# Feed-forward weights rounded in the key and value stage instead of the first cross-attention

## The chip, the core and the metric

The kernel runs on one core of one Trainium2 chip. The metric is device time in microseconds (us) from the start to the end of one execution; a kernel's time is the median of its runs.

## What is computed

The reference takes `x` (256 tokens of 1024) and a context of 4096 tokens, and adds six sublayers to `x`: a cross-attention to the context and the tokens (16 query heads, 4 key heads of width 96), a causal self-attention, a small routed layer, a second cross-attention to the context (32 heads of 32), a second causal self-attention, and a feed-forward layer on whole numbers. Only the last one's weights matter here:

```python
def _quant_w(W):
    ws = jnp.max(jnp.abs(W), axis=1, keepdims=True) / QMAX
    ws = jnp.maximum(ws, 1e-08)
    Wq = jnp.clip(jnp.round(W / ws), -QMAX, QMAX)
    return (Wq, ws)
...
gate = jnp.einsum('td,id->ti', q, Wgq) * s * wsg.T
up = jnp.einsum('td,id->ti', q, Wuq) * s * wsu.T
h = jax.nn.silu(gate) * up
q2, s2 = _quant_act(h)
out = jnp.einsum('ti,di->td', q2, Wdq) * s2 * wsd.T
```

`Wg` and `Wu` are 2752 x 1024, `Wd` is 1024 x 2752, all float32. Each row has its own scale, and the rows must be divided by it and rounded. The matmuls need the rounded weights turned (contraction on the partitions). None of this depends on `x`, so it can be done at any time before the last stage.

## The kernel before

**Key and value stage** (`latent_stage`). After the queries of the first cross-attention (16 heads, L416) come 17 chunks of 256 tokens. For each, PE multiplies the chunk by the key and value weights, each float32 operand split into a high and a low part, so three matmuls for each product (L449 to L451 for keys, L468 for values), and between them scores each finished key tile against the queries once, in the high part only, for the row maxima (L436). DVE takes the maxima (L601) and the low parts of keys (L614) and values (L623, L631); ACT takes the high parts (L547, L558). At a chunk's start ACT and DVE split the next chunk's context (`c_high` L489, `c_low` L499). `chunk_steps` is one list of steps that all engines walk through, each doing its own part: "mm" and "vmm" are matmul steps, "k" and "v" take a finished tile out of PSUM, "max" is a score and its maximum. The SP queue issues every transfer, strictly in that order: two context loads (L663, four `staged` tiles in turn), four key stores after each of the first two key tiles and two after the third (L685 to L692), three value stores after each of two value tiles (L698, L701). `bank_read`, counted by DVE, tells PE that a PSUM bank is free, and SP that a tile may be stored. POOL does nothing here.

**First cross-attention** (`cross_stage`). 136 steps, 34 for each of 4 key heads. In a step PE does six matmuls of scores (`scores`, L809 to L811) and six that weigh the values (`weigh`, L824 to L826); ACT computes two exponentials (L862, L863), DVE the low part of the probabilities (`probs_low`, L900). After each head DVE inverts the sums and normalises (`normalise`, L909 to L919), in the middle of its queue. Beside this the feed-forward weights are rounded, by the table `quant`: rows of 128 are loaded (`load_rows`, L1036), DVE finds each row's largest value (`find_top`, L941, and for `Wd` L947 and L933) and its scale and inverse (L925, L927), POOL multiplies and rounds in two passes (L1008, L1014), PE turns the result in 128 x 128 pieces (`turn`, L839), DVE copies them out of PSUM (`copy_turned`, L964) and SP spills them to scratch memory (`spill`, L1045 to L1051). In the last steps four units of the output projection's weights are split (L260, L265).

**Feed-forward stage** (`whole_number_stage`). Six chunks of gate and up weights, 512 wide and the last 192, are read back (`sp_chunk`, L2045, L2049) into two buffers, then multiplied for two tiles of tokens (`gate_and_up`, L2123); `down` is read back at once (L2278) and used by `project` (L2149).

## Time and profile before

| | us |
|---|---|
| median of 3 runs (2109.82 to 2115.65) | 2112.91 |
| the profiled execution | 2105.75 |
| its span, first to last instruction | 2104.4 |
| busy in the span: PE | 1920.4 (91%) |
| DVE | 1287.9 (61%) |
| ACT | 859.5 (41%) |
| POOL | 547.6 (26%) |
| DMA, mean rate | 123 GB/s |

The key and value stage runs from about 80 to 656 us of the span, the first cross-attention from 662.7 to 1093.2 us, the feed-forward stage from about 2010 us to the end. PE's busy time counts modelled, overlapping ends of matmuls, so the distance from one start to the next tells more than a duration. "Releaser" is what an engine waited for last. The granted clock is PE's, 1.00 for full speed. The trace of a DMA has its issue on the SP queue and its landing.

### The profile page before, as it was taken

To read this page: it belongs to the slowest core of one execution; us is meant where nothing else is said; L and a number is where in the kernel's file an instruction comes from. 1 tells how busy PE (TensorE), PEld (TensorE's weight loads), DVE (VectorE), ACT (ScalarE), POOL (GpSimd) and SP (SyncE) were. 2 spreads that over 40 slices of the span, in tenths; PEclk is the share of its full clock that TensorE was granted. 3 is DMA by queue.
4 is the path that set the end of the run, shared out by engine and by line. 5 is a ranking of instruction groups with operands and counts; after the bars stand their busy time and mean duration, and the time that the engine had idled before them with its cause. 6 is when DMAs were issued, how large, how long until landed. Compare 5 with 4: busy or idle time off the path is not lost.

```text
span 2104.4 us, 29620 instructions
## 1 busy us (share of the span) xinstructions
PE 1920.4 (91%) x11932; PEld 1411.2 (67%) x11932; DVE 1287.9 (61%) x1590; ACT 859.5 (41%) x1409; POOL 547.6 (26%) x264
## 2 busy tenths in 40 slices
PE   7899999999997999999998995779999999978977
PEld 5799999999996877787776874423333333366843
DVE  3445444454544787889965855667777775266465
ACT  2211111111113666666663451046777777535421
POOL 0000000000001555554510001036777777510000
PEclk9999999999998999999999998879999999999889
DMA  4533434343326666565724516523433420135052
GB/s 173 173 105 106 125 95 117 98 123 89 88 76 177 203 201 195 189 210 189 237 73 152 188 43 160 125 80 78 96 81 81 94 61 1 38 117 224 1 189 74
DMA packets 154808, 259.30 MB, mean 123 GB/s; under 512 B 36477, under 2 KB 102321, under 8 KB 147505
## 3 DMA queue, kind: packets, MB, share of 16 engines
q1 hardware_dynamic: 154673, 257.42, 40.6%
q8 instruction: 95, 1.56, 0.3%
q14 instruction: 40, 0.33, 0.1%
HBM read 192.39 MB, written 61.76 MB: 121 GB/s over the span
## 4 chain that ended last, share of the span: by engine, by line
PE 81%; DVE 11%; ACT 3%; issue 3%; DMA 2%; SPq 0%; POOL 0%; ACTq 0%; DVEq 0%
PE psum L468 10%; PE psum L1699 7%; PE psum L1716 5%; PE psum L449 4%; PE psum L451 4%; PE psum L450 4%; PE psum L436 3%; DVE top L1888 3%; PE psum L278 3%; PE psum L279 3%; PE psum L280 3%; PE psum L1732 3%; PE psum L809 3%; PE psum L1680 3%; PE psum L811 3%; PE psum L810 3%
## 5 line engine op out<-in xcount | busy, mean ns | idle before, releaser
L1888 DVE TENSOR_REDUCE top<-psum 128x4 f32<-128x2048 f32 x128 | 293.0, 2289 | 118.5 <-PE psum L1680 118.3
L1958 POOL TENSOR_TENSOR added<-probs_f 128x1024 f32<-128x1024 f32 x126 | 299.0, 2375 | 193.6 <-ACT probs_f L1815 141.8
L1815 ACT ACTIVATE probs_f<-psum 128x512 f32<-128x512 f32 x512 | 278.4, 594 | 139.3 <-PE psum L1699 127.1
L601 DVE TENSOR_REDUCE top<-psum 128x2 f32<-128x512 f32 x272 | 186.4, 691 | 198.3 <-PE psum L436 198.2
L900 DVE TENSOR_TENSOR probs_low<-probs,probs_high 128x1024 fp32r<-128x1024 f32 x136 | 195.1, 1438 | 79.1 <-ACT probs L863 78.9
L862 ACT ACTIVATE probs_high<-psum 128x1024 fp32r<-128x1024 f32 x136 | 139.9, 1029 | 160.0 <-PE psum L811 150.3
L1699 PE MATMUL psum<-q_rows,k_rows 97*128 97x512 f32 x512 | 197.5, 461 | 0.7 <-ACT probs_f L1815 0.5
L1699 PEld LDWEIGHTS psum<-q_rows,k_rows 97*128 97x128 f32 x512 | 80.7, 191 | 171.6 <-ACT probs_f L1815 159.1
L449 PE MATMUL psum<-c_high,w_high 128*128 128x256 f32 (+1 forms) x672 | 191.4, 285 | 3.2 <-issue 3.2
L450 PE MATMUL psum<-c_low,w_high 128*128 128x256 f32 (+1 forms) x672 | 191.3, 285 | 0.0
L451 PE MATMUL psum<-c_high,w_low 128*128 128x256 f32 (+1 forms) x672 | 191.0, 284 | 0.0
L1008 POOL TENSOR_SCALAR wf_rows<-wf_rows,w_inverse 128x1024 f32<-128x1024 f32 (+2 forms) x52 | 128.8, 2477 | 186.0 <-DVE w_inverse L927 186.0
L1001 POOL MEMSET key_high<- 1x512 f32 x4 | 1.9, 520 | 653.7 <-DVE top_low L637 653.7
L1716 PE MATMUL psum<-probs_f,v_pair 128*32 128x512 f32 x1024 | 139.9, 619 | 0.2 <-ACT probs_f L1815 0.2
L863 ACT ACTIVATE probs<-psum 128x1024 f32<-128x1024 f32 x136 | 138.5, 1018 | 0.0
L449 PEld LDWEIGHTS psum<-c_high,w_high 128*128 128x128 f32 (+1 forms) x672 | 129.1, 192 | 3.6 <-issue 3.6
L450 PEld LDWEIGHTS psum<-c_low,w_high 128*128 128x128 f32 (+1 forms) x672 | 129.2, 192 | 0.0
L451 PEld LDWEIGHTS psum<-c_high,w_low 128*128 128x128 f32 (+1 forms) x672 | 129.1, 192 | 0.0
L468 PE MATMUL psum<-w_high,c_high 128*128 128x384 f32 (+1 forms) x528 | 122.4, 310 | 0.0
L468 PE MATMUL psum<-w_high,c_low 128*128 128x384 f32 (+1 forms) x528 | 122.0, 309 | 0.0
L468 PE MATMUL psum<-w_low,c_high 128*128 128x384 f32 (+1 forms) x528 | 121.9, 309 | 0.0
L809 PE MATMUL psum<-q_high,key_high 97*128 97x512 f32 x272 | 114.1, 420 | 8.3 <-DMA value_low<-v_low 8.3
(357 smaller groups left out, 3806.3 us busy)
## 6 DMA issues: line engine op xcount, KB each, us to landing
wf_rows<-in_ffn_w_dram SPq DMA_DIRECT2D x42, 512.0 KB, 4.2
staged<-in_ctxT_dram SPq DMA_DIRECT2D x32, 512.0 KB, 4.7
k_four<-k_high SPq DMA_DIRECT2D x128, 128.0 KB, 3.3
wf_rows<-in_ffn_w_dram SPq DMA_DIRECT2D x8, 1376.0 KB, 7.4
q_dram<-wf_turned SPq DMA_DIRECT2D x42, 256.0 KB, 2.3
gate_up<-q_dram SPq DMA_DIRECT2D x10, 1024.0 KB, 8.1
value_high<-v_high SPq DMA_DIRECT2D x32, 256.0 KB, 3.6
value_low<-v_low SPq DMA_DIRECT2D x32, 256.0 KB, 4.3
```

Source lines behind the costliest of these rows:

```text
L449: pe.matmul(o, w_high[:, k, col:col + m], high[:, k, :], start=k == 0, stop=False)
L450: pe.matmul(o, w_high[:, k, col:col + m], low[:, k, :], start=False, stop=False)
L451: last = pe.matmul(o, w_low[:, k, col:col + m], high[:, k, :], start=False, stop=k == KT - 1)
L468: last = pe.matmul(o, tokens[:, k, ts], weights[:, k, cols], start=k == 0 and tokens is high and weights is w_high, stop=k == KT - 1 and t ...
L601: dve.tensor_reduce(top0[:, r0:r0 + 2, n], psum[:, bank, :].rearrange("p (i n) -> p i n", i=2), AX_X, ALU.max).then_inc(*b.bank_read.up())
L809: pe.matmul(o, key_high[slot][:, at], q_high[:, q], start=True, stop=False)
L900: dve.tensor_tensor(probs_low[n % 3][:], probs[n % 2][:], probs_high[n % 3][:].bitcast(F32), ALU.subtract).then_inc(*c.low_set.up())
L1699: pe.matmul(psum[:, half, :], k_rows[kv % 2][:, sn * P:(sn + 1) * P], q_rows[kv % 2][:, half * BANK:(half + 1) * BANK], start=True, stop=T ...
L1716: done = pe.matmul(psum[row:row + HD1, PRODUCTS, :], value, probs[:, (2 * pair + e) % 6, half * BANK:(half + 1) * BANK], start=p == 0, sto ...
L1815: act.activation(probs[:, n % 6, half * BANK:(half + 1) * BANK], psum[:, half, :], ACT.Exp, scale=scale).then_inc(*f.exped.up())
L1888: dve.tensor_reduce(top1[:, :, t, chunk], psum[:, MAXIMA:MAXIMA + G1, :], AX_X, ALU.max).then_inc(*f.max_read.up())
L1958: pool.tensor_tensor(added[pair % 4][:], probs[:, n % 6, :], probs[:, (n + 1) % 6, :], ALU.add).then_inc(*f.added.up())
```

## The change

The rounding moves from the first cross-attention to chunks 1 to 15 of the key and value stage. The host now also passes the three weight matrices turned (`ffn_t0` to `ffn_t2`). The row layout is still read, for the largest values only; the turned layout is read a second time, multiplied and rounded where it lies, so PE has nothing to turn and DVE nothing to copy.

- `SLOTS` puts six "find" and six "settle" steps into each of these chunks. At "find" DVE reduces one row tile (68 in all: 44 of `Wg` and `Wu`, 8 x 3 pieces of `Wd`) and SP spills a finished pair. At "settle" ACT does two passes on one pair of turned blocks, 128 x 1024 (70 in all, 15 slots behind the row tiles: `LAG`), and SP loads row tile i + 2 and pair i - 13. A pair's buffer is one of three (two new ones and `staged[2]`), so each turned load waits until the spill of three pairs before has landed.
- The inverses are needed along the free dimension now. They go out to scratch memory with one 4-byte element at a time and come back spread over all partitions, 14 times, into `staged[3]`. POOL multiplies each pair by them (one pass instead of two).
- Context loads have only `staged[0]` and `staged[1]` left, so they are issued one chunk later than before.
- To make room, the low part of the queries is kept in `c_high1` and `c_low1` at first, sent to scratch memory (2 x 768 KB) and loaded back in the last chunk. ACT's split of chunk 1 waits for that send.
- In the first cross-attention all rounding is gone, and the four early weight units are split at steps 120, 124, 128 and 132.
- Scratch layouts are what the last stage reads: each half of a gate and up chunk is one piece of up to 8 KB for each partition; the last chunk's matmuls are 192 wide instead of 128 and 64.

```diff
-    q_dram = scratch("q_dram", [2 * FT, P, KT * P], BF16)
-    qd_dram = scratch("qd_dram", [KT, P, FT * P], BF16)
+    q_low_dram = scratch("q_low_dram", [HD0, H0 * T], F32)
+    inverse_dram = scratch("inverse_dram", [NQ, P], F32)
+    q_dram = scratch("q_dram", [2, -(-FF // BANK), P, KT, BANK], BF16)
+    qd_dram = scratch("qd_dram", [P, FT, D], BF16)
...
-        q_low = sb(attn0, "q_low", [HD0 + 1, H0 * T], F32R)
...
+            rows = [sb(phase, f"wf_rows{i}", [P, D]) for i in range(2)]
+            turned = [sb(phase, f"wf_turned{i}", [P, 2 * BANK]) for i in range(2)]
+            parts = sb(phase, "wf_parts", [P, 2, 4, 3])
...
+            turned.append(staged[2][:, 0:2 * BANK])
+            inverses = [staged[3][:, i * BANK:(i + 1) * BANK] for i in range(2)]
+            wf_in, wt_in = (b.wf_in0, b.wf_in1), (b.wt_in0, b.wt_in1, b.wt_in2)
+            spilled = (b.spilled0, b.spilled1, b.spilled2)
+            q_low_parts = [z[1].rearrange("p k n -> p (k n)") for z in (c_high, c_low)]
...
+                z = i % 2 if what == "c" and i >= 2 else n % 4
...
+            blocks = [(0, 0), (1, 0), (2, 0), (0, 1), (1, 1), (2, 1)] + [(z, i) for i in range(2, chunks) for z in range(2)]
+            tops, top_end, pairs, pair_start = [], [], [], []
+            for z, i in blocks:
+                for tile in range(4 * i, min(4 * i + 4, KT if z == 2 else FT)):
+                    tops += [(z, tile, part) for part in range(3 if z == 2 else 1)]
+                top_end.append(len(tops) - 1)
+                pair_start.append(len(pairs))
+                pairs += [(len(top_end) - 1, z, i, m) for m in range((FT if z == 2 else KT) // 2)]
+            LAG = 15
...
+            SLOTS = {("mm", 0, 0, 0): "find", ("mm", 0, 0, 5): "settle", ("mm", 0, 1, 1): "find",
+                     ("mm", 1, 0, 0): "settle", ("mm", 1, 1, 0): "find", ("mm", 2, 0, 0): "settle",
+                     ("mm", 2, 0, 2): "find", ("vmm", 0, 0, 0): "settle", ("vmm", 0, 0, 3): "find",
+                     ("vmm", 1, 0, 0): "settle", ("vmm", 1, 0, 2): "find", ("vmm", 1, 0, 5): "settle"}
...
+                slotted, slot = [], (n - 1) * len(SLOTS) // 2
+                for step in steps:
+                    if step in SLOTS:
+                        slotted.append((SLOTS[step], slot, 0, 0))
+                        slot += SLOTS[step] == "settle"
+                    slotted.append(step)
+                return slotted
...
+                if n == 1:
+                    act.wait_ge(*b.q_low_sent.at(32))
...
+                def settle(r):
+                    z = width_of(*pairs[r][1:3])
+                    wide = turned[r % 3][:, 0:2 * z]
+                    act.wait_ge(*b.scaled.at(r + 1))
+                    act.activation(wide, wide, ACT.Copy, bias=ROUND).then_inc(*b.shifted.up())
+                    act.wait_ge(*b.shifted.at(r + 1))
+                    act.activation(turned[r % 3].bitcast(BF16)[:, 0:2 * z], wide, ACT.Copy,
+                                   bias=-ROUND).then_inc(*b.rounded.up())
...
+                        if what == "settle" and 0 <= i - LAG < len(pairs):
+                            settle(i - LAG)
...
+                    dve.wait_ge(*wf_in[m % 2].at(16 * (m // 2 + 1)))
+                    dve.tensor_reduce(top, rows[m % 2][0:height, 0:cols], AX_X, ALU.max,
+                                      apply_absolute_value=True).then_inc(*b.topped.up())
...
+                    n0, count = row_columns(z, i)
+                    top, scale, inverse = (t[:, n0:n0 + count] for t in (w_top, w_scale, w_inverse))
+                    dve.wait_ge(*b.topped.now())
+                    if z == 2:
+                        dve.tensor_reduce(top, parts[:, i], AX_X, ALU.max).then_inc(*s.small.up())
+                        dve.wait_ge(*s.small.now())
+                    dve.tensor_scalar(scale, top, 1.0 / QMAX, 1e-8, ALU.mult, ALU.max).then_inc(*s.small.up())
+                    dve.wait_ge(*s.small.now())
+                    dve.reciprocal(inverse, scale).then_inc(*b.inverted.up())
...
+                    dve.tensor_tensor(q_low_parts[h // 8][0:HD0, own], psum[0:HD0, 4 + h % 4, 0:T],
...
+                for r, (block, z, i, m) in enumerate(pairs):
+                    width = width_of(z, i)
+                    both = turned[r % 3][:, 0:2 * width].rearrange("p (z n) -> p z n", z=2)
+                    if m == 0:
+                        pool.wait_ge(*b.inverse_in.at(16 * (block + 1)))
+                    pool.wait_ge(*wt_in[r % 3].at(16 * (r // 3 + 1)))
+                    pool.tensor_tensor(both, both, inverses[block % 2][:, 0:width].unsqueeze(1).broadcast_to([P, 2, width]),
+                                       ALU.mult).then_inc(*b.scaled.up())
...
+                        sp.wait_ge(*b.topped.at(m - 1))
+                    sp.dma_start(rows[m % 2][0:height, 0:cols],
+                                 a[f"ffn_w{z}"][tile * P:tile * P + height, first:first + cols]).then_inc(*wf_in[m % 2].up(16))
...
+                    if r >= 3:
+                        sp.wait_ge(*spilled[r % 3].at(16 * (r // 3)))
...
+                    sp.dma_start(turned[r % 3][:, 0:2 * width].rearrange("p (z n) -> p z n", z=2),
+                                 turned_place(a[f"ffn_t{z}"].rearrange("(k p) n -> p k n", p=P), z, i, m)).then_inc(
+                                     *wt_in[r % 3].up(16))
+                def spill(r):
+                    _, z, i, m = pairs[r]
+                    width = width_of(z, i)
+                    destination = (turned_place(qd_dram, z, i, m) if z == 2
+                                   else q_dram[z, i, :, 2 * m:2 * m + 2, 0:width])
+                    sp.wait_ge(*b.rounded.at(r + 1))
+                    sp.dma_start(destination, turned[r % 3].bitcast(BF16)[:, 0:2 * width].rearrange(
+                        "p (z n) -> p z n", z=2)).then_inc(*spilled[r % 3].up(16))
...
+                    sp.wait_ge(*b.inverted.at(block + 1))
+                    sp.dma_start(inverse_dram[n0:n0 + count, :].rearrange("n p -> p n"),
+                                 w_inverse[:, n0:n0 + count],
...
+                        sp.wait_ge(*b.scaled.at(pair_start[block - 1]))
+                    sp.dma_start(inverses[block % 2][:, 0:width],
+                                 inverse_dram.rearrange("n p -> (n p)")[n0 * P:n0 * P + width].partition_broadcast(P)
...
+                    loaded = place["c", 3] + 1
+                    for n in range(loaded):
+                        load(n)
+                    for i, part in enumerate(q_low_parts):
+                        sp.wait_ge(*b.q_split.at(8 * i + 8))
+                        sp.dma_start(q_low_dram[:, i * 8 * T:(i + 1) * 8 * T],
+                                     part[0:HD0, :].bitcast(F32)).then_inc(*b.q_low_sent.up(16))
...
+                        if what == "find":
+                            if 0 <= i - LAG - 1 < len(pairs):
+                                spill(i - LAG - 1)
+                        elif what == "settle":
+                            if i + 2 < len(tops):
+                                load_rows(i + 2)
+                            if i in top_end:
+                                send_inverses(top_end.index(i))
+                            if i - LAG + 2 in pair_start:
+                                load_inverses(pair_start.index(i - LAG + 2))
+                            if 0 <= i - LAG + 2 < len(pairs):
+                                load_turned(i - LAG + 2)
...
+                sp.dma_start(q_low[0:HD0, :].bitcast(F32), q_low_dram).then_inc(*b.q_low_in.up(16))
...
+            q_low = sb(attn0, "q_low", [HD0 + 1, H0 * T], F32R)
+            place_queries()
+            sync_program(range(LATENTS, NCH))
+            place_tops()
...
-                    for what, m, first, last in quant[n]:
-                        if what == "turn":
-                            turn(m, first, last)
...
-                    if n >= quantised_at and unit < ahead_in_cross:
-                        if unit == 0:
-                            act.wait_ge(*c.spilled0.now())
-                            act.wait_ge(*c.spilled1.now())
+                    if n in split_after:
...
-                    for what, m, first, last in quant[n]:
-                        if what == "turn":
-                            copy_turned(m, first, last)
-                        elif what == "top":
-                            find_top(m)
-                        elif what == "top first":
-                            find_top_first(m)
...
+            width = min(BANK, FF - i * BANK)
...
+                tile = gate_up[i % 2][:, which, 0:KT * width].rearrange("p (k n) -> p k n", n=width)
+                sp.dma_start(tile, q_dram[which, i, :, :, 0:width]).then_inc(*chunk_in[i % 2].up(16))
...
+            down = sb(phase, "down", [P, FT, D], BF16)
...
+                        for k in range(KT):
+                            done = pe.matmul(psum[:, bank, 0:width], intsT[:, k, t * P:(t + 1) * P],
+                                             gate_up[i % 2][:, which, k * width:(k + 1) * width], start=k == 0,
+                                             stop=k == KT - 1)
...
+                sp.dma_start(down[:], qd_dram).then_inc(*ffn.down_in.up(16))
...
+    a["ffn_t0"], a["ffn_t1"] = c(i["L1_ffn_Wg"].T), c(i["L1_ffn_Wu"].T)
+    a["ffn_t2"] = np.pad(i["L1_ffn_Wd"].T, ((0, 64), (0, 0)))
```

Three places show how instructions move. Here `wf_turned` and `staged` are the pair buffers, `in_ffn_t` the turned weights, `in_ffn_w` the rows.

The SP queue at the start of a chunk of the key and value stage, before:

```order
L698 DMA v_low<-v_out1l 128x4x128
L701 DMA v_dram<-v_out 128x256
L663 DMA staged<-in_ctxT_dram 128x1024 [waits latent_c_split] x2
L685 DMA k_high<-k_out0h 96x2x256 [waits latent_bank_read]
L688 DMA k_high<-k_out0h 32x2x256
L685 DMA k_low<-k_out0l 96x2x256
L688 DMA k_low<-k_out0l 32x2x256
L685 DMA k_high<-k_out1h 96x2x256 [waits latent_bank_read]
L688 DMA k_high<-k_out1h 32x2x256
```

The same place now, in a chunk in which all three streams run:

```order
L774 DMA staged<-in_ctxT_dram 128x1024 [waits latent_c_split] x2
L807 DMA qd_dram<-staged 128x2x512 [waits latent_rounded]
L782 DMA wf_rows<-in_ffn_w_dram 128x1024 [waits latent_topped]
L797 DMA staged<-in_ffn_t_dram 128x2x512 [waits latent_spilled2]
L807 DMA qd_dram<-wf_turned 128x2x512 [waits latent_rounded]
L869 DMA k_high<-k_out0h 96x2x256 [waits latent_bank_read]
L872 DMA k_high<-k_out0h 32x2x256
L869 DMA k_low<-k_out0l 96x2x256
L872 DMA k_low<-k_out0l 32x2x256
L782 DMA wf_rows<-in_ffn_w_dram 128x1024 [waits latent_topped]
L797 DMA wf_turned<-in_ffn_t_dram 128x2x512 [waits latent_spilled0]
L807 DMA qd_dram<-wf_turned 128x2x512 [waits latent_rounded]
```

Each `L797` waits for the spill issued three pairs before it, and the key stores of `k_out0h` now stand behind two spills, a row load and such a wait.

ACT in one chunk of that stage, before:

```order
L489 ACTIVATE c_high<-staged 128x1024 [waits latent_stage_in0,latent_made]
L489 ACTIVATE c_high<-staged 128x1024 [waits latent_stage_in1,latent_made]
L547 ACTIVATE k_out0h<-psum 128x512 [waits latent_k_sent0,latent_made]
L547 ACTIVATE k_out1h<-psum 128x512 [waits latent_k_sent1,latent_made]
L547 ACTIVATE k_out2h<-psum 128x256 [waits latent_k_sent2,latent_made]
```

And now:

```order
L548 ACTIVATE c_high<-staged 128x1024 [waits latent_stage_in0,latent_made]
L548 ACTIVATE c_high<-staged 128x1024 [waits latent_stage_in1,latent_made]
L575 ACTIVATE wf_turned<-wf_turned 128x1024 [waits latent_scaled]
L577 ACTIVATE wf_turned<-wf_turned 128x1024 [waits latent_shifted]
L617 ACTIVATE k_out0h<-psum 128x512 [waits latent_k_sent0,latent_made]
L575 ACTIVATE wf_turned<-wf_turned 128x1024 [waits latent_scaled]
L577 ACTIVATE wf_turned<-wf_turned 128x1024 [waits latent_shifted]
L617 ACTIVATE k_out1h<-psum 128x512 [waits latent_k_sent1,latent_made]
L575 ACTIVATE staged<-staged 128x1024 [waits latent_scaled]
L577 ACTIVATE staged<-staged 128x1024 [waits latent_shifted]
L617 ACTIVATE k_out2h<-psum 128x256 [waits latent_k_sent2,latent_made]
L575 ACTIVATE wf_turned<-wf_turned 128x1024 [waits latent_scaled]
```

Between any two reads of PSUM there are now one or two pairs of rounding passes, and the first of each waits for POOL.

PE in the first cross-attention, between two steps, before:

```order
L824 MATMUL psum<-probs_high,value_high 128x512
L825 MATMUL psum<-probs_low,value_high 128x512
L826 MATMUL psum<-probs_high,value_low 128x512
L839 MATMUL psum<-ident_b,wf_ints 128x128 [waits cross_group_copied,cross_rounded]
L839 MATMUL psum<-ident_b,wf_ints 128x128 x7
L809 MATMUL psum<-q_high,key_high 128x512 [waits cross_exped]
L810 MATMUL psum<-q_low,key_high 128x512
L811 MATMUL psum<-q_high,key_low 128x512
```

And now:

```order
L981 MATMUL psum<-probs_high,value_high 128x512
L982 MATMUL psum<-probs_low,value_high 128x512
L983 MATMUL psum<-probs_high,value_low 128x512
L966 MATMUL psum<-q_high,key_high 128x512 [waits cross_exped,cross_kv_in2]
L967 MATMUL psum<-q_low,key_high 128x512
L968 MATMUL psum<-q_high,key_low 128x512
```

The eight transposes between the steps, with their waits, are gone; nothing takes their place.

## Rows read from the trace of the kernel before

**Rows 1.** Windows: stretch, length, busy time (instructions) of each engine, clock, DMA share, GB/s.
```profile
300.00:400.00 100.00, 96.86 (x732) 95.55 (x732) 49.62 (x74) 13.27 (x21) 0.00 (x0) 1.00 0.38 111
784.00:876.00 92.00, 92.00 (x487) 73.63 (x485) 74.03 (x94) 59.32 (x62) 54.04 (x32) 1.00 0.64 203
1000.00:1050.00 50.00, 50.00 (x278) 39.87 (x277) 45.00 (x50) 30.80 (x32) 30.45 (x8) 1.00 0.72 241
4.00:10.00 6.00, 0.00 (x0) 0.00 (x0) 3.74 (x12) 1.80 (x3) 0.00 (x0) 1.00 0.98 389
658.00:688.00 30.00, 25.28 (x106) 20.21 (x107) 14.33 (x15) 16.91 (x18) 6.26 (x4) 0.85 1.00 283
880.00:890.00 10.00, 9.41 (x39) 6.97 (x39) 9.73 (x15) 3.47 (x5) 2.70 (x1) 0.83 0.30 99
```

**Rows 2.** Chain that ended last, key and value stage: start, length, what.
```profile
270.94 1.76 PE psum L468 x12
...
304.83 1.76 PE psum L468 x12
```

**Rows 3.** PE's timeline, first cross-attention: start, length, instruction.
```profile
702.53 0.62 PE L839 MATMUL psum<-ident_b,wf_ints 128*128 128x128 bf16 x8
...
705.80 0.40 PE L809 MATMUL psum<-q_high,key_high 97*128 97x512 f32 x1
...
708.57 0.62 PE L839 MATMUL psum<-ident_b,wf_ints 128*128 128x128 bf16 x8
```

**Rows 4.** The same timeline where `Wd` is turned.
```profile
1064.97 1.07 PE L839 MATMUL psum<-ident_b,wf_ints 128*128 128x128 bf16 x16
...
1068.69 0.40 PE L809 MATMUL psum<-q_high,key_high 97*128 97x512 f32 x1
...
1074.91 0.40 PE L809 MATMUL psum<-q_high,key_high 97*128 97x512 f32 x1
```

**Rows 5.** DVE's timeline behind the first head's `normalise`.
```profile
777.65 0.69 DVE L964 COPY wf_turned<-psum 128x1024 bf16<-128x1024 bf16 x1
...
779.77 2.34 DVE L900 TENSOR_TENSOR probs_low<-probs,probs_high 128x1024 fp32r<-128x1024 f32 x2
```

**Rows 6.** PE's timeline at the same place; in brackets idle time and releaser.
```profile
781.03 0.50 PE L824 MATMUL psum<-probs_high,value_high 128*128 128x512 f32 x1 [1.41 <-DVE probs_low L900]
```

**Rows 7.** ACT's timeline in one chunk of the key and value stage.
```profile
287.17 2.00 ACT L489 ACTIVATE c_high<-staged 128x1024 fp32r<-128x1024 f32 x2
292.53 0.60 ACT L547 ACTIVATE k_out0h<-psum 128x512 fp32r<-128x512 f32 x1 [3.36 <-PE psum L451]
299.90 0.60 ACT L547 ACTIVATE k_out1h<-psum 128x512 fp32r<-128x512 f32 x1 [6.78 <-PE psum L451]
303.74 0.39 ACT L547 ACTIVATE k_out2h<-psum 128x256 fp32r<-128x256 f32 x1 [3.24 <-PE psum L451]
```

**Rows 8.** Lines view by shape, DVE: count, busy us, mean ns, idle before.
```profile
L941 DVE TENSOR_REDUCE w_top<-wf_rows 128x1 f32<-128x1024 f32 x42 | 50.6, 1205 | 1.3 <-DMA wf_rows<-in_ffn_w_dram 1.3
```

**Rows 9.** Costliest groups of the page, POOL.
```profile
L1958 POOL TENSOR_TENSOR added<-probs_f 128x1024 f32<-128x1024 f32 x126 | 299.0, 2375 | 193.6 <-ACT probs_f L1815 141.8
```

**Rows 10.** Timeline of POOL and DVE late in the first cross-attention.
```profile
1039.06 3.47 POOL L1008 TENSOR_SCALAR wf_rows<-wf_rows,w_inverse 128x2752 f32<-128x2752 f32 x1 [4.07 <-DVE w_inverse L927]
...
1040.33 3.27 DVE L900 TENSOR_TENSOR probs_low<-probs,probs_high 128x1024 fp32r<-128x1024 f32 x1 [0.24 <-ACT probs L863]
```

**Rows 11.** DMA issues of the page: count, KB each, median us to landing.
```profile
staged<-in_ctxT_dram SPq DMA_DIRECT2D x32, 512.0 KB, 4.7
...
q_dram<-wf_turned SPq DMA_DIRECT2D x42, 256.0 KB, 2.3
gate_up<-q_dram SPq DMA_DIRECT2D x10, 1024.0 KB, 8.1
```

**Rows 12.** Timeline around the start of chunk 0.
```profile
78.98 1.49 DVE L583 TENSOR_TENSOR w_low<-staged,w_high 128x1280 fp32r<-128x1280 f32 x1 [0.74 <-ACT w_high L523]
...
89.27 0.60 ACT L547 ACTIVATE k_out0h<-psum 128x512 fp32r<-128x512 f32 x1 [8.42 <-PE psum L451]
```

291 lines of the change are left out of this document (94 added, 197 removed).

## The prediction

> **What bounds the kernel now.** I read the windows first, for who is full in each stage. In the key and value stage PE is: busy 96.9 of 100 us at full clock, with DVE at 49.6, ACT at 13.3, POOL at nothing and the DMA engines at 0.38 of their time, 111 GB/s [rows 1]. The chain of waits repeats the same PE step every 304.83 − 270.94 = 33.89 us, one chunk, so nothing but PE sets that period [rows 2]. In the first cross-attention PE fills its window too, but DVE (74 of 92), ACT (59) and POOL (54) are loaded and the DMA engines are at 0.64 [rows 1]. PE's timeline there shows what it is full of: matmul steps and transposes in turn [rows 3]. The change takes work from a stage where PE is the bound and puts none on PE. What it loads instead in the other stage is ACT, DVE, POOL and above all the DMA engines; the question is what they still hide.
>
> **What goes in the cross-attention.** From eight transposes to the next score matmul is 705.80 − 702.53 = 3.27 us, from there to the next transposes, a step without any, 708.57 − 705.80 = 2.77 [rows 3]. So `turn` costs 0.50 us, 44 times for `Wg` and `Wu`: 22 us. For `Wd`, sixteen transposes lengthen a part to 1068.69 − 1064.97 = 3.72, by 0.95, and the next six make 1074.91 − 1068.69 − 2.77 = 3.45, by 0.68 [rows 4]; 1.63 × 8 row tiles = 13 us. Together −35; nothing else then fills a step, since two exponentials on ACT and one `probs_low` are shorter than 2.77 us. At a head's end PE waits 1.41 us for `probs_low` [rows 6], which stood behind a copy out of PSUM, a maximum and scales, from 777.65 to 779.77, or 2.1 us of DVE [rows 5]. All that goes. There are three such boundaries and I take −7 for them (from −4, the 1.41 three times, to −10).
>
> POOL's rounding goes as well. One `probs_low` took 3.27 us: it started at 1040.33 while POOL's pass ran from 1039.06 to 1042.53, and ended 1.07 us after it, where two unhindered ones take 2.34 [rows 5, 10]. It was held for as long as POOL went on. PE had steps in hand there, so I count nothing for it beyond the −7.
>
> **What is added in the key and value stage.**
> - ACT: 70 pairs of passes. A pass over 128 x 1024 is 1.0 us (two take 2.00), so 2.0 us for each settle, in gaps of 3.36, 6.78 and 3.24 us between its reads of PSUM, with longer ones behind the third [rows 7]. Hidden, if POOL has been in time. If a pass is late, `k_out0h` is late, then its bank, and PE waits at a score or key matmul.
> - DVE: 68 maxima at 1.205 us [rows 8], 6 a chunk: 7.2 us beside 16.8 (0.496 × 33.9), 24 of 33.9. Hidden.
> - POOL: 70 multiplies of 128 x 1024, nearest row 2.375 us [rows 9], one per slot of 33.9 / 6 = 5.65. Hidden.
> - A pair's buffer is free again after load 4.7, multiply 2.4, passes 2.0, spill 2.3 [rows 7, 9, 11]: 11.4 us, against three slots, 16.9. Spare time is 5.5 us, and it is the loads that will eat it.
> - DMA: a slot moves 0.52 MB of rows, 0.52 MB turned and 0.26 MB spilled, six slots 7.9 MB; with the short blocks I take 7.6. The old traffic takes 0.38 × 33.9 = 12.9 us of DMA time. What 7.6 MB take no row shows, so I bound it by rates per full share [rows 1]: weight loads with nothing else 389 / 0.98 = 397 GB/s, 19.1 us; the cross-attention, which has just such loads and spills, 203 / 0.64 = 317 and 241 / 0.72 = 335; the crowded turn of the stages 283, 26.9 us. The cross-attention is nearest: 326 gives 23.3 + 12.9 = 36.2 us, more than a chunk has. The DMA engines become the bound by 2.3 us a chunk. All three streams run together in slots 15 to 67, 9 chunks: **+21 us**, with ends 0 (32.0 us, still hidden) and +53 (39.8).
> - SP: 36 issues a chunk where there were 18, in strict order, with six waits for a spill to land (2.3 us each at best [rows 11]). Here a late transfer turns into a wait of others: behind such a wait stand key stores, and the next context and row loads. Once the DMA is full this is how PE comes to wait; while it isn't, 6 × 2.3 = 14 us of 33.9 is affordable. Not counted twice.
> - Inverses: 14 sends of up to 512 single elements, each followed by a load. The tightest pair is one slot apart, 5.65 us; no row has such a send. Between nothing and a few us each time; I take 0 and leave the rest to the range.
>
> **The start of the stage.** `q_low` (1.57 MB) can only be sent after the last weight split, 78.98 + 1.49 = 80.47, and 1.05 MB of context share the DMA engines with it: 2.6 MB at 326 GB/s is 8 us, plus a landing, so about 91; then ACT splits chunk 1 (2.00 us [rows 7]) ahead of `k_out0h`, which stood at 89.27 [rows 12]. I take **+4** (0, if it goes at 397 and PE has banks in hand, to +8).
>
> **The rest.** In the feed-forward stage 32 matmuls fewer, each 78 ns as the eight transposes in 0.62 [rows 3], about −1 after their columns; its loads are as large as before, 8.1 us [rows 11]: −1, between −3 and +2. Clock: at the second head's end a wait of PE was followed by a granted clock of 0.83 over 10 us [rows 1], 1.7 us lost at most; new waits may bring more such stretches, gone ones fewer: +1 (−2 to +15).
>
> **Sum.** −35 − 7 + 21 + 4 − 1 + 1 = **−17**. The profiled execution has 2105.75, so 2089 for one like it. That execution is 7.2 below the median; 2112.91 − 17 = 2096.
>
> **A rule to weigh.** The Trainium skill, "DMA: Bandwidth & Descriptors", section Specifications, gives a limit of about 358 GB/s between HBM and one core. By that figure, as an estimate, the added traffic takes 21.2 us and a chunk 34.1: nearly hidden, a term of +2 for +21, and 2077 in all. Its "Where 436 GB/s comes from" calls this the per-core limit; this trace had 389 GB/s on six us [rows 1], so it disagrees upwards.
>
> **Rivals.**
> - A, the transfers keep up. At 362 GB/s or more (7.6 MB in 33.9 − 12.9 us) the chunk stays near 33.9. For it: 389 GB/s has been seen. Against: every stretch with mixed loads and stores gave 283 to 335. −35 − 7 + 4 − 1 = −39, 2074. Chance 0.27.
> - C, slower. If mixed small packets keep the rate at 283, a chunk is 39.8 us: +53, the start +8, the clock +3, less 43: +21 at most; with the start at +4 and the clock at +1, +15, **2128**. It decides at chunks longer by (43 − 4 − 1) / 9 = 4.2 us, 38.1 us, or 302 GB/s: the rates of the cross-attention are only 5 to 10% above that. In its favour: stores to scratch are in pieces of 1 KB, and SP's strict order adds waits to full engines. Chance 0.20.
> - D, POOL and DVE take turns. If POOL held DVE in all it does, as it held `probs_low` [rows 10], the chunk would need 24.0 + 6 × 2.375 = 38.3 us, +4.4 × 11.7 chunks = +51, in place of the +21: 2126. Against it: DVE 74 and POOL 54 fit into 92 us [rows 1], and the maxima, among them, average 1205 ns [rows 8]. I believe in it only for `c_low`, two a chunk, which has slack. Chance 0.03. The Trainium skill, "SBUF — State Buffer", section Who interferes with whom, says the same of DVE instructions with two inputs from SBUF, and that `tensor_reduce` never contends; the row agrees on the first (held 2.1 us).
> - E, the transfers are late enough to give back about what the transposes gave, 37 to 38 us a chunk: 2107 to 2119, chance 0.05 beside the forecast's own 0.45.
>
> **How the numbers follow.** What can be told from no change is about 0.3%, 6.3 us. Faster: all of A, 0.39 of the forecast's 0.45 (its own range 2084 to 2112): 0.66. Within 0.3%: 0.06 of the forecast, 0.04 of E, 0.03 of C: 0.13. Slower: 0.17 of C, 0.03 of D, 0.01 of E: 0.21. The range goes from 2066 (A with −10 at the boundaries and a faster end) to 2128 (C, D).
>
> **What would show it.** PE's steps of the cross-attention 2.77 us apart throughout, and no wait of 1.41 at a head's end: right for −42. The same key matmul of chunks 5 to 12: 34 us apart is A, 36 the forecast, 38 E, 40 C. If 36 or more, DMA share near 1, DVE's maxima waiting for `wf_rows`, ACT's passes for POOL, POOL for a turned load; if the share is well under 1 and SP waits for spills instead, the bound is the order of the queue, and my sum by rates is wrong though its size might fit. If maxima take much over 1.2 us while POOL works, it is D. `k_out0h` of chunk 0 near 93 instead of 89 shows the start. A granted clock under 1 in the stage would make all of it wrong.

## The result and the profile after

| | before | changed |
|---|---|---|
| median | 2111.37 us (4 runs) | 2191.34 us (4 runs, 2182.66 to 2205.47) |
| ratio | | 1.0393 [1.0348, 1.0438] |
| the profiled execution | 2105.75 | 2198.19 |
| its span | 2104.4 | 2196.9 |

Slower by 80 us, where 17 less were forecast. The two profiled executions lie 92 us apart, since the one before is 6 us below its median and the changed one 7 us above. The windows, before and then after, tell the stage (columns as in [rows 1]):

```profile
240.00:640.00 400.00, 387.42 (x2927) 382.18 (x2926) 194.73 (x292) 51.19 (x81) 0.00 (x0) 1.00 0.34 98
662.00:1093.00 431.00, 420.18 (x2160) 333.58 (x2161) 348.26 (x418) 273.02 (x286) 212.71 (x104) 0.99 0.61 197
1093.00:2104.40 1011.40, 886.09 (x5357) 487.12 (x5355) 629.75 (x708) 490.02 (x974) 332.03 (x147) 0.94 0.34 98
```

```profile
240.00:640.00 400.00, 306.40 (x2059) 299.39 (x2059) 202.34 (x281) 138.85 (x158) 121.85 (x51) 0.88 0.87 240
793.00:1185.00 392.00, 385.22 (x1629) 311.88 (x1630) 191.50 (x170) 272.34 (x285) 0.00 (x0) 0.98 0.29 85
1185.00:2196.90 1011.90, 888.58 (x5321) 490.32 (x5325) 630.40 (x708) 490.93 (x974) 332.08 (x147) 0.93 0.35 99
```

The cross-attention begins at 793.6 instead of 662.7, **+131 us**, and takes 392.3 instead of 430.7 from its first score matmul to the end of its last value matmul, **−38**; what follows is the same to within half a microsecond. 130.9 − 38.4 is the 92.5 by which the spans differ. So the key and value stage lost nearly all of it: in the same 400 us PE made 2059 matmuls, not 2927.

PE's timeline after, in the cross-attention: steps of 2.77 us where 3.27 and 2.77 alternated before [rows 3], and at a head's end what is left of the waits:

```profile
884.73 0.40 PE L966 MATMUL psum<-q_high,key_high 97*128 97x512 f32 x1
...
887.50 0.40 PE L966 MATMUL psum<-q_high,key_high 97*128 97x512 f32 x1
...
895.96 0.47 PE L981 MATMUL psum<-probs_high,value_high 128*128 128x512 f32 x1 [1.36 <-DVE sums L321]
```

The same timeline in the key and value stage, the first value matmul of chunks 4 and 5: 54.3 us apart, against 33.89 before [rows 2].

```profile
241.97 0.46 PE L525 MATMUL psum<-w_high,c_high 128*128 128x384 f32 x2
...
296.29 0.70 PE L525 MATMUL psum<-w_high,c_high 128*128 128x384 f32 x2
```

Taken so for every chunk, the distances from chunk 0 on are 33.7, 33.7, 34.1, 34.4, then, from chunk 4 on (the first turned load is issued at 200.7, in chunk 3), 54.3, 43.6, 39.9, 47.2, 51.6, 44.3, 54.3, 44.1, 45.2, 38.4, and 33.7 again. The ten long ones are 124 us over ten of 33.9. Some 6 of the rest came before: chunk 0's first value matmul is at 106.0 instead of 100.2.

The engines are not what holds them. The instructions of the rounding took what they had been given (view of each line, ns min/median/max):

```profile
L644 DVE TENSOR_REDUCE w_top<-wf_rows x44: 1200/1217/1222, 126.8 to 608.7; 128x1 f32<-128x1024 f32 x42, 64x1 f32<-64x1024 f32 x2
...
L748 POOL TENSOR_TENSOR wf_turned<-wf_turned,staged x47: 1004/2387/3208, 207.3 to 719.1; 128x1024 f32<-128x1024 f32 x42, 128x384 f32<-128x384 f32 x5
...
L575 ACT ACTIVATE wf_turned<-wf_turned x47: 515/1058/1064, 209.7 to 724.2; 128x1024 f32<-128x1024 f32 x42, 128x384 f32<-128x384 f32 x5
```

What does is in the chain of waits (start, length, what): a row load that takes 11.76 us to land, for which DVE waits with a maximum, and a spill that takes 12.92, with the next turned load behind it.

```profile
238.45 11.76 DMA wf_rows<-in_ffn_w_dram
250.20 0.02 issue
250.22 1.22 DVE w_top L644
...
276.14 12.92 DMA qd_dram<-staged
289.06 0.02 issue
289.08 0.38 SPq L797
```

The row load was issued half a microsecond ahead of a send of inverses (238.92), the spill nine behind one (267.00). The waits of the SP queue, from 240 to 700 us (total, times, longest), say who stood still for such landings: the turned loads, 205 us in all.

```profile
SPq L797 <- DMA q_dram<-wf_turned: 72.3, 22, 9.0
SPq L797 <- DMA q_dram<-staged: 60.1, 13, 11.1
SPq L797 <- DMA qd_dram<-wf_turned: 42.1, 14, 7.7
SPq L797 <- DMA qd_dram<-staged: 30.5, 7, 7.4
```

DVE stood still too, for row loads (L644, whole kernel; total, times):

```profile
  DMA wf_rows<-in_ffn_w_dram: 126.2, 33
```

Both ways lead to PE: from 240 to 640 us it waited 33.5 us for `k_out0h` from ACT and 49.3 for `k_out1l` and `k_out2l` from DVE.

And the sends themselves: 9.1 to 13.0 us from issue to landing. Around the one at 303.26 the windows show others held: 335 GB/s, then 54 over eight microseconds, then 309.

```profile
303.00:307.00 4.00, 4.00 (x30) 4.00 (x29) 2.52 (x4) 0.87 (x1) 2.29 (x1) 1.00 1.05 335
307.00:315.00 8.00, 7.38 (x52) 7.11 (x51) 4.11 (x7) 2.49 (x3) 0.10 (x1) 1.00 0.56 54
315.00:319.00 4.00, 4.00 (x35) 4.00 (x34) 0.69 (x1) 0.00 (x0) 1.95 (x1) 1.00 0.93 309
```

The view of the send's line (L813) ends with this:

```profile
DMA to landing us min/median/max: 9.1/11.8/13.0
```

The three theories were: **S**, the element-wise sends; **Q**, three buffers and one strictly ordered queue; **R**, bytes against a rate, which was the forecast's own term.

### The profile page after: what moved, and what is told of

Read it like the earlier page. It is cut to its first block, busy times and chain, and to the rows that moved or that the text cites. A ratio compares the mean times of both kernels' runs of the same rounds, so it can differ in the third digit from the quotient of the medians.

```text
span 2196.9 us, 28458 instructions
## 1 busy us (share of the span) xinstructions
PE 1925.0 (88%) x11366; PEld 1425.7 (65%) x11372; DVE 1216.9 (55%) x1440; ACT 994.8 (45%) x1549; POOL 493.1 (22%) x231
## 4 chain that ended last, share of the span: by engine, by line
PE 65%; DMA 16%; DVE 11%; ACT 3%; issue 3%; SPq 1%; POOL 1%; ACTq 0%; DVEq 0%; POOLq 0%
PE psum L1732 7%; PE psum L525 5%; PE psum L1749 5%; DVE top L1921 3%; PE psum L281 3%; DMA q_dram<-staged 3%; PE psum L282 3%; PE psum L283 3%; PE psum L966 3%; PE psum L968 3%; PE psum L967 3%; PE psum L981 3%; PE psum L1765 3%; PE psum L982 3%; PE psum L983 3%
## 5 line engine op out<-in xcount | busy, mean ns | idle before, releaser
L1991 POOL TENSOR_TENSOR added<-probs_f 128x1024 f32<-128x1024 f32 x126 | 299.1, 2375 | 193.2 <-ACT probs_f L1848 145.4
L1035 DVE TENSOR_TENSOR probs_low<-probs,probs_high 128x1024 fp32r<-128x1024 f32 x136 | 166.6, 1226 | 207.1 <-ACT probs L1001 207.1
L506 PE MATMUL psum<-c_high,w_high 128*128 128x256 f32 (+1 forms) x672 | 197.3, 294 | 3.2 <-issue 3.2
L748 POOL TENSOR_TENSOR wf_turned<-wf_turned,staged 128x1024 f32<-128x1024 f32 (+1 forms) x47 | 107.4, 2284 | 410.2 <-DMA wf_turned<-in_ffn_t_dram 410.2
L507 PE MATMUL psum<-c_low,w_high 128*128 128x256 f32 (+1 forms) x672 | 197.2, 293 | 0.0
L508 PE MATMUL psum<-c_high,w_low 128*128 128x256 f32 (+1 forms) x672 | 196.5, 292 | 0.0
L506 PEld LDWEIGHTS psum<-c_high,w_high 128*128 128x128 f32 (+1 forms) x672 | 135.0, 201 | 3.6 <-issue 3.6
L507 PEld LDWEIGHTS psum<-c_low,w_high 128*128 128x128 f32 (+1 forms) x672 | 135.3, 201 | 0.0
L508 PEld LDWEIGHTS psum<-c_high,w_low 128*128 128x128 f32 (+1 forms) x672 | 135.3, 201 | 0.0
L525 PE MATMUL psum<-w_high,c_high 128*128 128x384 f32 (+1 forms) x528 | 128.9, 325 | 0.0
L493 PE MATMUL psum<-k_out0h,q_high 96*128 96x256 f32 x272 | 61.0, 308 | 62.0 <-ACT k_out0h L617 40.9
```

Of the source, the lines that this page charges most:

```text
L506: pe.matmul(o, w_high[:, k, col:col + m], high[:, k, :], start=k == 0, stop=False)
L507: pe.matmul(o, w_high[:, k, col:col + m], low[:, k, :], start=False, stop=False)
L508: last = pe.matmul(o, w_low[:, k, col:col + m], high[:, k, :], start=False, stop=k == KT - 1)
L525: last = pe.matmul(o, tokens[:, k, ts], weights[:, k, cols], start=k == 0 and tokens is high and weights is w_high, stop=k == KT - 1 and t ...
L1035: dve.tensor_tensor(probs_low[n % 3][:], probs[n % 2][:], probs_high[n % 3][:].bitcast(F32), ALU.subtract).then_inc(*c.low_set.up())
L1991: pool.tensor_tensor(added[pair % 4][:], probs[:, n % 6, :], probs[:, (n + 1) % 6, :], ALU.add).then_inc(*f.added.up())
```

## Experiments

"Changed" is the changed kernel. Ratios are to the kernel before, run in between on the same chip; its median was 2106 to 2108 us there, and 1.0393 corresponds to 2190. Gains are differences of medians; chunk lengths and windows are those of one profiled execution, which can lie up to 11 us from its median.

**e1.** DVE turns the inverses so that 32 lie in a row:

```diff
-                    dve.reciprocal(inverse, scale).then_inc(*b.inverted.up())
+                    dve.reciprocal(inverse, scale).then_inc(*s.small.up())
...
+                    dve.transpose(inv_rows[block % 2][:], w_inverse[:, n0:n0 + 32]).then_inc(*b.inverted.up())
...
-                    sp.dma_start(inverse_dram[n0:n0 + count, :].rearrange("n p -> p n"), w_inverse[:, n0:n0 + count],
-                                 allow_slow_non_contiguous=True).then_inc(*b.inverse_sent.up(16))
+                    for q in range(4):
+                        sp.dma_start(inverse_dram[n0:n0 + count, 32 * q:32 * q + 32],
+                                     inv_rows[block % 2][32 * q:32 * q + count, :]).then_inc(...)
```

> Edit: DVE turns the inverses in 32 x 32 blocks, so that each send is four transfers with 128-byte runs instead of one with up to 512 single elements; everything else as in the change. Three theories for the 124 us that chunks 4 to 13 gained. S (sends): an element-wise send takes 9.1 to 13.0 us to land and holds the spills and loads behind it in the same queues. Then these sends land in 2 to 4 us and the kernel gains most of it: 60 to 90 us, to 2100 to 2130. Q (cycle of three buffers in one strict queue): a pair's buffer comes back too late whatever the sends do: gain 10 to 30 us. R (rate): the bytes are the same, gain under 5 us.

Measured 2126.0 us, 1.0091 [1.0059, 1.0123]: 65 us gained, as S had it. The chunks from 4 on are 41.2, 40.3, 39.8, 43.0, 38.7, 41.2, 41.4, 36.8, 37.6, 35.2: the ones of 54 are gone, but none is at 34.

**e2.** No row loads after the first two.

```diff
                     if m >= 2:
-                        sp.wait_ge(*b.topped.at(m - 1))
+                        return
```

> Edit: only the first two row tiles are loaded, DVE reduces the same two buffers again and again; leaves out 66 row loads (34 MB), so all inverses but the first ones are those of other rows. R: 3.1 MB of the 7.6 MB a chunk go, at 283 to 326 GB/s 10 us a chunk: chunks come back to about 34 us, gain 95 to 120 us. Q: spills and turned loads land sooner, by 1 to 2 us each, chunks of 37 to 40 us, gain 50 to 80. S: the sends stay at 9 to 13 us, gain under 30.

Measured 2160.3 us, 1.0272 [1.0231, 1.0314], 31 us gained: a microsecond above what S allowed, and against R, by which two fifths of the added bytes fewer should have given back nearly everything. With the sends in place the chunks from 4 to 12 still took 34.7 to 50.6 us.

**e3.** A fourth pair buffer: `turned[r % 3]` becomes `turned[r % 4]`, and so the flags and waits.

> Edit: a fourth pair buffer (room from a trimmed k_out2 and from v1_out placed in the unused ends of staged[2] and staged[3]); a load waits for the spill of four pairs before, issued one and a half slots ago instead of half a slot. Q: 205 us of SP's waits for spills nearly vanish, gain 70 to 110 us, to about 2090 to 2120. R: DMA engines stay full, gain under 10. S: a send's 9 to 13 us are covered in part by the spare buffer, gain 20 to 50.

Measured 2140.1 us, 1.0154 [1.0116, 1.0192], 51 us gained. That is the upper end of what S allowed (20 to 50) and short of Q: a spare buffer rides over a part of each hole.

**e4.** Turned and inverse loads half a slot later (in SP's "find" step, behind the spill).

> Edit: turned loads and inverse loads are issued half a slot later, right behind the spill of that slot, so SP waits for a spill issued a full slot before instead of half a slot. Q: SP's strict order is the cost: fewer waits, but POOL gets its pair half a slot later; gain 20 to 50 us. R: no change within 5 us. S: gain under 10 us. If the cycle itself (load, multiply, passes, spill) is longer than three slots, it stays at zero or gets worse.

Measured 2173.8 us, 1.0309 [1.0281, 1.0336], 17 us gained: more than S had allowed (under 10), a little less than Q had asked (20). The place in SP's order is a small part.

**e5.** e1 and e3 together.

> Edit: e1 (sends with 128-byte runs) and e3 (four buffers) together. Each alone took 65 and 51 us off the changed kernel. If the sends and the short cycle were the whole of it, chunks come back to 34 us and the time is what the prediction's rival A gave, 2070 to 2080. If behind them the DMA engines are the bound (share 0.88 at 282 GB/s in e1), chunks stay at 36 to 38 us and the time at 2090 to 2110.

Measured 2109.4 us, 1.0000 [0.9985, 1.0016]: another 17 us on e1, and exactly level with before. Chunks 4 to 11 are 38.2 us on average (37.9 with chunk 12), the second branch of the expectation. What still holds PE is in the chain, which passes seven times between 234 and 546 us through a row load of over 5 us; here the one ahead of PE's score at 284.05:

```profile
270.00 1.18 SPq L880
...
272.66 7.33 DMA wf_rows<-in_ffn_w_dram
...
280.01 1.23 DVE w_top L645
```

SP hardly waits for spills there (3.4 us), but DVE stood for row loads 43.7 us between 240 and 640 us (total, times, longest):

```profile
DVE w_top L645 <- DMA wf_rows<-in_ffn_w_dram: 28.9, 14, 4.6
DVE wf_parts L645 <- DMA wf_rows<-in_ffn_w_dram: 14.8, 5, 4.9
```

**e6.** e5 without the row loads.

> Edit: e5 and without the row loads after the first two (leaves out 66 row loads, the inverses are those of other rows). If bytes bound e5, this one has chunks of 33.9 us and is at 2065 to 2080; if e5 is already there, the same as e5 within 5 us; if something else than transfers holds the stage (DVE, POOL, the passes on ACT), no better than e5 although that is above 2090.

Measured 2076.3 us, 0.9828 [0.9802, 0.9854]. The chunks are at 33.7 to 35.2 us, and the time where rival A stood. So the third branch is out: with the sends and the buffers mended, DVE, POOL and ACT hide all of their work, and what is left of the loss, 33 us, hangs on the row loads. Whether by their bytes or by DVE's waits for their landing the run doesn't tell, since it takes both away: here DVE never waits for a row. A third row buffer would have parted the two; it was not run. The windows of e5 and e6 beside each other:

```profile
240.00:640.00 400.00, 363.40 (x2662) 355.84 (x2661) 263.52 (x351) 173.32 (x206) 144.62 (x64) 0.97 0.87 277
```

```profile
240.00:640.00 400.00, 385.50 (x2913) 379.12 (x2912) 270.74 (x374) 175.59 (x211) 146.16 (x65) 1.00 0.74 228
```

**e7.** The changed kernel with each send made twice, one behind the other, the second to another scratch tensor.

> Edit: the changed kernel, with each element-wise send made twice, the second to a scratch tensor that nobody reads. S: the price of a send is that of the traffic held behind it, 65 us for 14 sends by e1, so 14 more cost 40 to 90 us: 2220 to 2280. If e1 gained only because a load of inverses waited for its send to land, the second sends cost little: under 15 us.

Measured 2180.5 us, 1.0327 [1.0306, 1.0347]: not slower at all. This spoke against S as I had put it, that a send has a price per send. The trace showed a hole of the same length behind the pair as behind the single one (64 GB/s over eight microseconds from 305.0). Either the two holes coincide, or it was something else in e1 that gained. For the first speak the landings of the two sends, issued half a microsecond apart (first to the tensor that is read, then to the other), which are alike:

```profile
DMA to landing us min/median/max: 9.2/11.1/12.9
```

```profile
DMA to landing us min/median/max: 9.1/11.2/13.1
```

e9 was made to decide.

**e8.** e5 with the spills issued by ACT.

> Edit: e5, with the spills issued by ACT right behind its two passes instead of by SP. If SP's strict order still costs, this gains 5 to 20 us on e5. If the DMA engines or nothing bound e5, the same within 5 us; it could lose some, since an issue takes ACT's time ahead of the next read of PSUM.

Measured 2112.5 us, 1.0011 [0.9995, 1.0028]: the same as e5 within 3 us. That the spills stand in SP's order costs nothing more there; the loads still do stand in it.

**e9 and e10.** e1, and the element-wise send beside it, to a tensor that nobody reads: side by side as in the change, or each element 512 bytes from the next.

```diff
+                    sp.dma_start(spare_dram[n0:n0 + count, :].rearrange("n p -> p n"), w_inverse[:, n0:n0 + count], ...)
```

```diff
+                    sp.dma_start(spare_dram[n0:n0 + count, :, 0:1].rearrange("n p o -> p n o"),
+                                 w_inverse[:, n0:n0 + count].unsqueeze(2), ...)
```

> Edit: e1, and beside its four turned transfers the element-wise send is made as well, to a scratch tensor that nobody reads or waits for. In the changed kernel the DMA engines moved 350 GB/s before such a send and 20 to 100 GB/s from 4 to 12 us behind it, single packets taking 3 to 7 us, the same behind the doubled sends of e7. B (a send blocks the traffic for some 7 us, whoever waits for it): 14 x 5 us back, 2180 to 2195, as in the change. W (e1 gained because the load of the inverses no longer waited for a late landing): stays at e1's 2126, within 10 us.

> Edit: as e9, but the unread elements are written 512 bytes apart instead of side by side. B1 (what blocks is that up to 512 four-byte writes go to the same 2 KB of memory): the hole is gone or much shorter, 2126 to 2145. B2 (what blocks is the number of four-byte elements, read or written): the same as e9, 2180 or more. If e9 shows no cost, neither does this.

Measured 2201.2 us, 1.0437 [1.0415, 1.0459], for e9: 75 us for 14 sends on which nobody waits, 6 us above B's range and far from W. And 2131.4 us, 1.0102 [1.0081, 1.0123], for e10: 5 us, within the noise of e1's 1.0091. The number of elements, their size and the instruction are the same; only where they fall in memory differs. Windows around such a send, e9 (issued at 304.69) and e10 (289.81):

```profile
305.00:309.00 4.00, 4.00 (x29) 3.80 (x27) 1.99 (x4) 0.85 (x2) 2.15 (x1) 1.00 0.89 301
309.00:317.00 8.00, 7.37 (x52) 7.32 (x52) 4.53 (x7) 2.12 (x2) 0.22 (x1) 1.00 0.35 23
317.00:321.00 4.00, 4.00 (x36) 4.00 (x35) 0.00 (x0) 0.00 (x0) 2.19 (x1) 1.00 1.07 364
```

```profile
290.00:294.00 4.00, 4.00 (x18) 4.00 (x17) 1.76 (x2) 0.77 (x1) 2.37 (x1) 0.53 1.03 303
294.00:302.00 8.00, 7.37 (x52) 7.11 (x51) 4.10 (x6) 4.61 (x5) 2.39 (x1) 1.00 0.73 210
302.00:306.00 4.00, 4.00 (x32) 4.00 (x31) 1.74 (x3) 0.88 (x2) 1.20 (x1) 1.00 1.00 343
```

And the issues of each in the DMA view from 240 to 600 us (count, KB, median us to landing):

```profile
spare_dram<-w_inverse SPq DMA_DIRECT2D x10, 2.0 KB, 10.8
```

```profile
spare_dram<-w_inverse SPq DMA_DIRECT2D x10, 2.0 KB, 5.5
```

So S is shown in this form: up to 512 writes of four bytes into the same 2 KB hold nearly all other transfers for some eight microseconds. e7 fits with it: its two sends are under way at the same time and share one hole. Why they cost no more together was not tried.

**e11.** e5, slots in chunk 0 too and the rounding 25 slots behind instead of 15.

```diff
-            LAG = 15
+            LAG = 25
...
-                if n == 0 or n == LATENTS:
+                if n == LATENTS:
```

> Edit: e5 with slots in chunk 0 too and LAG 25 instead of 15, so that the row loads run alone for longer and all three streams overlap in slots 25 to 67 (7 chunks) instead of 15 to 67 (9 chunks). R (behind sends and buffers the bytes bound): chunks with all streams stay at 37 to 40 us but there are two fewer, gain 6 to 14 us on e5's 2109: 2095 to 2103, just faster than before. If it isn't the bytes, no gain.

Measured 2105.2 us (12 runs), 0.9984 [0.9972, 0.9995]: 4 us on e5, less than the 6 to 14. Of the versions that compute everything it is the only one whose interval lies below 1, ahead of the kernel before by 0.2%.

**e12.** e5 with eight maxima a chunk in chunks 0 to 3, then four.

> Edit: e5, with the row maxima spread otherwise: eight in each of chunks 0 to 3, where no turned load runs, then four a chunk instead of six; the first settle stands at chunk 4. A chunk with all streams then moves 6.6 MB instead of 7.6. R: at the 300 to 310 GB/s of e11's full stretches (share 0.94) such a chunk takes 34.5 to 35.5 us instead of 38 to 40: 2080 to 2095, faster than before by about 1%. If it isn't the bytes but the strict order of SP's queue, chunks stay at 37 us or more and the time at 2100 or above.

Measured 2105.7 us, 0.9984 [0.9965, 1.0003], above the 2080 to 2095. From chunk 4 on the chunks were 33.7 to 38.8, 35.4 on average, as R said; but chunks 0 to 3 went from 33.8 to 36.0 each, and the first value matmul of chunk 4 came at 252.0 instead of 240.1: 12 us lost ahead of the 21 that the ten chunks from 4 on gained. DVE's waits for row loads are down to 1.3 us between 240 and 640, so the shorter chunks don't tell bytes from waits either.

**e13 and e14.** Seven maxima a chunk and then four; six and then five, at places that had been free.

> Edit: as e12, but seven maxima a chunk instead of eight in chunks 0 to 3, at places of which six were free in e5 (chunks of 33.7 us), and SP issues the next row load half a slot behind a maximum, as in the change. Two causes can be behind e12's missing gain. F (front): its dense maxima lengthened chunks 0 to 3 to 36 us, which these don't: 34 us there, 35 us in chunks 4 to 13, 2090 to 2098. R2 (the bytes still cost as much wherever they are put): what the front gives back comes again later, 2102 or more.

> Edit: as e13, with six maxima a chunk in chunks 0 to 3 and five from chunk 4 on, 7.1 MB a chunk. F: chunks 0 to 3 at 33.7, chunks 4 to 12 at about 36: 2095 to 2102, between e13 and e11. R2: 2102 or more.

Measured 2115.3 us, 1.0024 [1.0000, 1.0048], and 2122.4 us, 1.0072 [1.0052, 1.0092]: both outside F and where R2 had them. But chunks 0 to 3 of e13 took 35.0 us, not 34, so F's premise was not met. In e13, with 6.6 MB a chunk like e12, chunks 5 to 8 took 41.3, 38.6, 37.9 and 42.6 us; in e14, with 7.1 MB, chunks 4 to 12 took 38.7 on average, where e5 with 7.6 MB had 37.9. Bytes per chunk therefore don't foretell a chunk's length.

**e15.** e11 with eight row tiles loaded and reduced while the queries are made.

> Edit: e11, with the first eight row tiles loaded and reduced while the queries are made, before chunk 0, where the DMA engines were at about half of their time; finds in the chunks end at slot 59 instead of 67. R: 4.2 MB leave the stretch with all streams; at 277 GB/s that is 15 us of transfers, of which the stretch gives back some 5 to 12: 2093 to 2101. If the query part itself is lengthened by the eight loads (its weights arrive later), the gain is given back there: 2102 to 2108.

Measured 2106.0 us, 0.9988 [0.9972, 1.0005], no gain on e11, the second branch: chunk 0's first value matmul came at 109.3 instead of 106.6, and the chunks with all streams stayed at 35 to 40 us.

What these layouts have in common is the rate over the 400 us. e11, e12, e13:

```profile
240.00:640.00 400.00, 368.30 (x2712) 361.25 (x2711) 257.19 (x346) 179.00 (x208) 152.40 (x67) 0.97 0.87 277
```

```profile
240.00:640.00 400.00, 377.14 (x2816) 370.04 (x2817) 257.76 (x348) 182.58 (x216) 156.02 (x69) 0.99 0.87 275
```

```profile
240.00:640.00 400.00, 366.50 (x2684) 360.54 (x2683) 253.39 (x338) 176.85 (x206) 161.16 (x66) 0.97 0.85 274
```

From e11 to e15 and in e5 it is 270 to 277 GB/s at a share of 0.85 to 0.87, whichever way the loads are laid. But these 400 us reach past the chunks in which all streams run. For e5 the windows apart are:

```profile
240.00:546.00 306.00, 273.35 (x1988) 267.35 (x1987) 216.09 (x284) 134.67 (x152) 115.95 (x48) 0.97 0.93 302
```

```profile
546.00:640.00 94.00, 90.05 (x676) 88.48 (x676) 47.42 (x68) 38.66 (x54) 28.67 (x17) 1.00 0.66 196
```

302 / 0.93 = 325 GB/s at full share is the forecast's 326; the share was 0.93 and not 1. Whether DVE's waits for rows, other landings that come one by one, PE's own pace between the waits, or the memory keeps it there stays open.

## Why the prediction was wrong

**The cross-attention** was right in its main term. The steps are 2.77 us everywhere, and the stage shrank by 38 us, forecast 42. What is lacking is at the heads' ends. I had taken the wait for `probs_low` [rows 6] three times over; the trace of before has it at the first end only, with 2.06 us for the copied transposes at the third and neither at the second:

```profile
993.62 0.62 PE L839 MATMUL psum<-ident_b,wf_ints 128*128 128x128 bf16 x6 [2.06 <-DVE wf_turned L964]
```

What is left at all three, 1.2 to 1.4 and 0.6 us of PE for DVE's sums, was there before as well and stayed. The rows of one place are not those of three.

**The engines** were right: 1217 ns for 1205, 2387 for 2375, 1058 for 1000, and e6 shows all of it hidden. Rival D is out: maxima beside POOL have a longest of 1222 ns. The rule on the shared port in the Trainium skill ("SBUF — State Buffer", Who interferes with whom), that `tensor_reduce` never contends, agrees with that row. `probs_low` was also held no more: its longest is 1227 ns, with POOL idle there. `c_low`, of which the forecast said that it has slack, was held by POOL: up to 3453 ns for a median of 1225, and the longest ended at 557.14, 1.08 us after the multiply beside it. In e5 it makes 12.7% of the chain from 240 to 546 us, so it had no slack there; in e6, where it is held as long, the chunks are short all the same.

**The start** was right in mechanism, and 6 us instead of 4. ACT's wait ended when `q_low` had landed, at 90.9 (about 91 forecast), and PE stood 3.96 us:

```profile
80.04 1.49 DVE L677 TENSOR_TENSOR w_low<-staged,w_high 128x1280 fp32r<-128x1280 f32 x1 [0.74 <-ACT w_high L591]
...
90.90 2.00 ACT L548 ACTIVATE c_high<-staged 128x1024 fp32r<-128x1024 f32 x2 [10.89 <-DMA q_low_dram<-c_low]
...
93.44 0.80 PE L493 MATMUL psum<-k_out0h,q_high 96*128 96x256 f32 x2 [3.96 <-ACT k_out0h L617]
```

**The rest** was right: between 0 and +0.5 for −1.

**The step that failed is "Inverses: … Between nothing and a few us each time; I take 0 and leave the rest to the range."** A send costs 65 / 14 = 4.6 us by e1, 75 / 14 = 5.4 us by e9. "A few", read as five, even held, but that upper end, 14 × 5 = 70 us, never went into the range or into rival C, which I had built from rates alone. And I had priced it as a thing that only its own reader waits for (the pair one slot apart), not as one that stops everybody. I took 0 with no row to lean on, against the one thing that was plain in the diff, single elements of four bytes.

**The second step is the spare time of the buffer cycle, 5.5 us.** It was worked out from landings in a quieter stage, 4.7 and 2.3 us; in the full one a turned load still takes 4.7 at the median but up to 12.8, and a spill 5.4 and up to 13.0. The medians make 4.7 + 2.4 + 2.1 + 5.4 = 14.6 us against 16.9, which leaves 2.3 us of spare time, and a late landing goes straight through to the passes on ACT, `k_out0h` and PE. The row loads (6.0 us at the median, up to 13.3, into two buffers) had no such sum in the forecast at all, and DVE's 126 us of waits were for them. "Not counted twice" was the wrong call for SP's waits: they were a cost of their own, 17 us behind the mended sends (e5 against e1), 51 with the holes in place (e3).

**The third is the term of the row, turned and spilled bytes, +21 us.** e6 against e5 gives 33 for the row loads, and e5's chunks are 38.2 us where 36.2 stood. The rate was right (325 GB/s at full share for 326); the share of full use that I assumed, 1, was 0.93 in e5. That bytes at this rate are what sets the length is argued, not shown: by e6 it can as well be DVE's waits for rows, and e13 and e14 speak against bytes alone.

Put together: −38 in the cross-attention, +6 at the start, +65 sends, +17 cycle, +33 row loads are +83; measured +80. The first two are from the profiled pair, the others from medians. In this sum the clock has no term of its own, since it comes with the waits; in the 54 us from chunk 10's first value matmul to chunk 11's, PE was busy for 39.4 us with 249 matmuls; before, 732 took 96.86 at full clock [rows 1], so 249 take 33:

```profile
523.00:577.00 54.00, 39.42 (x249) 38.52 (x248) 25.42 (x33) 16.88 (x20) 15.12 (x7) 0.84 0.89 226
```

About six and a half of these 20 extra microseconds are the lower granted clock. My +1 for it (up to +15) was far too small once PE was stalled in every chunk.

Rival C named the right side and, in passing, the right kind of evidence (small stores, SP's order), but its mechanism, the engines full at 283 GB/s, is not what happened, and its 2128 was 63 us short. Its threshold came out all the same: chunks of 38.1 us over nine chunks were to make the two kernels equal, and e5, with 37.9 over nine, is level. The 358 GB/s of the Trainium skill ("DMA: Bandwidth & Descriptors", Specifications), by which the stage would have been nearly hidden, was not reached over a long stretch: 278 GB/s (e8) is the most that any layout held over 400 us, and 302 to 304 what e5 and e8 held over the 306 us with all streams.

## What to carry to other kernels

Price a transfer by what it does to those beside it, not by who waits for it: a send of 2 KB was the dearest thing in a change that moved 90 MB. A cost for which there is no row belongs into the range at its upper end times its count. And when a stage is to hide new transfers, work the buffer cycle out with landings from the busiest stretch of the trace, since those of a quiet one leave no room for the load that the change itself brings.
